# Two small router operations on VectorE move to the end of steps 5 and 7

## The reference, cut to what matters

```
x = x + window_attention(group_norm(x))     # 16 images of 256 tokens, 16 heads of 32
t = t + attention(layer_norm(t))            # the same 16 x 256 tokens, 8 heads of 16
t = t + experts(layer_norm(t))              # 8 experts, each token uses 2

# in experts, the router:
logits = x @ router_w.T + router_b
topk_val, topk_idx = top_k(logits, 2)
weights = softmax(topk_val)
onehot = one_hot(topk_idx, 8)
cw = einsum('btk,btke->bte', weights, onehot)
```

## Time and profile before

| | |
|---|---|
| median of 3 executions | 775.05 us (773.21 to 776.81) |
| the profiled execution | 776.03 us |
| its span, first to last instruction | 774.2 us |
| busy: PE, PEld, DVE, ACT, POOL | 646.9, 546.3, 515.2, 503.8, 483.6 us |
| mean granted TensorE clock | 0.953 of full speed |

### The profile page before, as it was taken

One profiled execution on the slowest core, in us unless ns is written; L12 is line 12 of the kernel. 1 busy time (PEld: TensorE's weight loads), 2 busy tenths in 40 slices (PEclk: granted clock), 3 DMA queues, 4 the chain that ended last, 5 costly groups with the idle time before them and its releaser, 6 DMA issues. The chain is left out here.

```text
span 774.2 us, 20293 instructions
## 1 busy us (share of the span) xinstructions
PE 646.9 (84%) x7070; PEld 546.3 (71%) x7070; DVE 515.2 (67%) x1513; ACT 503.8 (65%) x1427; POOL 483.6 (62%) x556
## 2 busy tenths in 40 slices
PE   3887989998989989899898999978884799999910
PEld 2766877877878778787787877767663688888800
DVE  4666768778787787887878878775342446565512
ACT  2555888778877788877888777765540256666600
POOL 5354656665868677686776767667365336666645
PEclk9799999999999999999999999999997789999965
DMA  7102113032230322303223031230732213233247
GB/s 202 29 3 35 17 21 96 11 91 35 76 98 25 91 42 82 89 34 92 42 82 87 30 97 36 85 83 36 206 122 97 65 43 93 87 88 88 73 137 215
DMA packets 54218, 59.27 MB, mean 77 GB/s; under 512 B 10370, under 2 KB 49410, under 8 KB 53602
## 3 DMA queue, kind: packets, MB, share of 16 engines
q1 hardware_dynamic: 44918, 45.65, 23.0%
q0 software_dynamic: 4544, 9.38, 3.4%
q10 hardware_dynamic: 4656, 2.95, 1.4%
HBM read 36.00 MB, written 28.64 MB: 83 GB/s over the span
## 5 line engine op out<-in xcount | busy, mean ns | idle before, releaser
L566 POOL TENSOR_TENSOR pb<-pb,rcb 128x512 f32<-128x512 f32 x128 | 155.5, 1215 | 151.7 <-DVE rcb L859 150.4
L614 POOL DMA_INDIRECT ysl<-yo,dst x78 | 75.4, 967 | 61.1 <-DVE yo L1133 44.4
L725 ACT ACTIVATE pb<-pSB,mxb 128x256 f32<-128x256 f32 x128 | 59.5, 469 | 46.4 <-DVE mxb L959 45.8
L725 ACT ACTIVATE pb<-pSA,mxb 128x256 f32<-128x256 f32 x128 | 59.6, 475 | 41.2 <-DVE mxb L959 41.2
L574 POOL TENSOR_TENSOR pa<-pa,rca 128x512 f32<-128x512 f32 x64 | 67.2, 1051 | 28.5 <-DVE rca L1024 28.5
L1252 PE MATMUL pTB<-ident,pb 128*128 128x128 f32 x512 | 79.4, 278 | 4.9 <-ACT ptb L739 4.8
L739 ACT ACTIVATE ptb<-pTB 128x512 f32<-128x512 f32 x128 | 77.1, 602 | 1.6 <-PE pTB L1252 1.6
L500 POOL DMA_INDIRECT slots<-rec,slot x64 | 65.3, 1020 | 13.8 <-issue 13.7
L745 ACT ACTIVATE pta<-pTA 128x512 f32<-128x512 f32 x64 | 38.6, 604 | 39.1 <-PE pTA L1344 38.6
L1252 PEld LDWEIGHTS pTB<-ident,pb 128*128 128x128 f32 x512 | 57.4, 141 | 9.0 <-issue 6.6
L959 DVE TENSOR_REDUCE mxb<-pSB 128x2 f32<-128x512 f32 x64 | 43.8, 685 | 20.3 <-PE pSB L1221 20.2
(11 more groups left out here) (221 smaller groups left out, 2015.3 us busy)
## 6 DMA issues: line engine op xcount, KB each, us to landing
slots<-sel_dram SPq DMA_DIRECT2D x16, 1040.0 KB
kbd<-kst SPq DMA_DIRECT2D x128, 64.0 KB, 2.4
xt<-slots SPq DMA_DIRECT2D x39, 130.0 KB, 2.2
xch<-x_ch_dram SPq DMA_DIRECT2D x4, 512.0 KB, 7.0
xt<-x_tok_dram SPq DMA_DIRECT2D x16, 128.0 KB, 2.4
xch<-t SPq DMA_DIRECT2D x16, 128.0 KB, 2.1
fw<-f_dram SPq DMA_DIRECT2D x1, 2048.0 KB
yc<-ysl SPq DMA_DIRECT2D x8, 256.0 KB, 9.4
```

What stands on the lines that cost most here:

```text
L566: pool.tensor_tensor(pb[:, b, :, :], pb[:, b, :, :], rcb[:, b, :].unsqueeze(2).to_broadcast([128, 2, TOK]), ALU.mult).then_inc(sb_nrm, 1)
L614: pool.indirect_dma_start(ysl, bass.IndirectOffsetOnAxis(ap=dst[:, t % YB, n:n + 1], axis=0), yo[:, t % YB, n, :], None).then_inc(y_dma[t ...
L725: last = a.activation(pb[:, b, qc, :], (pSB, pSA)[n % 2][:, qc * TOK:(qc + 1) * TOK], ACT.Exp, bias=mxb[:, b, qc:qc + 1], accum_out=smb[:, ...
```

## The change

On VectorE, in the function `iteration`, two blocks are moved and nothing else is touched. The comparison that makes `chose` stood at the start of step 5 and now stands at its end; the addition that makes `rden` stood at the start of step 7 and now stands at its end.

```
--- before.py
+++ after.py
@@ -875,16 +875,6 @@
                         for s in range(2):
                             last = v.max_index(ix8[:, s, :], mx8[:, s, :], lg[:, s, :])
                         last.then_inc(q_top, 1)
-                    if L is not None and n == 5:
-                        v.wait_ge(q_top, L.j * 3 + 2)
-                        if K is not None:
-                            v.wait_ge(q_mine, K.j + 1)
-                        v.tensor_tensor(chose[:, :, :, :], iota[:, :].unsqueeze(1).unsqueeze(1).to_broadcast([128, 2, 2, E]),
-                                        ix8[:, :, 0:2].rearrange("p s k -> p k s").unsqueeze(3).to_broadcast([128, 2, 2, E]),
-                                        ALU.is_equal).then_inc(q_top, 1)
-                    if L is not None and n == 7:
-                        v.wait_ge(q_exp, L.j + 1)
-                        v.tensor_scalar(rden[:, :, :], rexp[:, :, :], 1.0, None, ALU.add).then_inc(q_den, 1)
                     if K is not None and n == 0:
                         v.wait_ge(q_both, K.j + 1)
                         wait(v, q_pos, K.j)
@@ -1031,6 +1021,16 @@
                     if R is not None and n == 5:
                         v.wait_ge(r_ag, R.j + 1)
                         v.tensor_scalar(rs2[:, :], mv2[:, :, 1], EPS, None, ALU.add).then_inc(r_eps, 1)
+                    if L is not None and n == 5:
+                        v.wait_ge(q_top, L.j * 3 + 2)
+                        if K is not None:
+                            v.wait_ge(q_mine, K.j + 1)
+                        v.tensor_tensor(chose[:, :, :, :], iota[:, :].unsqueeze(1).unsqueeze(1).to_broadcast([128, 2, 2, E]),
+                                        ix8[:, :, 0:2].rearrange("p s k -> p k s").unsqueeze(3).to_broadcast([128, 2, 2, E]),
+                                        ALU.is_equal).then_inc(q_top, 1)
+                    if L is not None and n == 7:
+                        v.wait_ge(q_exp, L.j + 1)
+                        v.tensor_scalar(rden[:, :, :], rexp[:, :, :], 1.0, None, ALU.add).then_inc(q_den, 1)
```

## The result

| | before | changed |
|---|---|---|
| median | 774.48 us (22 runs) | 769.09 us (22 runs) |
| the profiled execution | 776.03 us | 765.13 us |
| its span | 774.2 us | 763.3 us |

The ratio to the kernel before is 0.9948, 95% interval 0.9931 to 0.9965: 4.0 us (2.7 to 5.3) of 774.5 are saved. One of the 22 executions of the kernel before took 1066.86 us and does not count in the ratio. 772.0 was forecast, 3.0 us less than the 775.05 of before, and "within 0.5%" as the likeliest; the measured ratio lies just beyond that edge, and its interval holds both sides of it.

The account below looks back on a forecast made before the run. VectorE's waits for GpSimd stall TensorE, but the key DMAs from `kst` to step 0 bound or nearly bound. 1.5 + 1.0 + 0.5 = 3.0 us off 776.03 gives 773.0, on the median 772.0; range 766 to 778.5.

Parts of the forecast that it names:

- within 0.5%: Whole kernel: a time not to be told from no change, between 771.2 and 778.9 us; chance 0.60.
- What bounds the kernel: VectorE's `chose` and `rden` wait for GpSimd; from `kst` to step 0 key DMAs bound or are within 0.4 us.
- Step 5, start: The cast inherits `chose`'s wait: 0.09 us gained per steady pass, 1.0 in all, and 0.5 in the first full pass.
- Step 5, end: `chose`, issued 0.01 to 0.02 us before GpSimd's next multiplication, gets through in about 0.17 us at no cost.
- Rival 3: End of step 5: `chose` waits for one multiplication (778 us, chance 0.08) or two (790 us, chance 0.05).
- Step 7: `q` starts earlier, TensorE regains 0.54 us a pass, but only the key DMAs' room of 1.5 us in sum counts.
- Step 0: `rden` pushes L893 to 0.02 us behind GpSimd's start; if caught it waits 1.04 us, hidden by the wait for TensorE.
- The sum: Whole kernel: 1.5 + 1.0 + 0.5 = 3.0 us saved, giving 772.0 us on the median.
- the forecast's own case: Whole kernel: 772.0 us, own range 770 to 774 from the late landings; chance 0.48.
- Rival 2: Step 0: key DMAs are not the bound in executions without late landings; 8.0 us saved, 767 us; chance 0.10.
- rival 1: Step 5: the cast does not exclude GpSimd, `kst` moves by some 0.8 us; 9.3 us saved, 766 us; chance 0.13.

Follow-up runs that it names:

- f3: The kernel before with four of the eight key DMAs, heads 4 to 7 getting no keys; ratio to the kernel before 0.9914.
- f4: The changed kernel with four of the eight key DMAs, heads 4 to 7 getting no keys; ratio to the kernel before 0.9786.
- g5: The changed kernel with the cast moved from step 5 into step 0 of the next pass, between the two sums; ratio to the kernel before 1.0078.
- h10: The changed kernel with the cast in step 0 of the next pass and `chose` in step 6 behind `tn`; ratio to the kernel before 0.9845.
- f2: The kernel before with only `chose` moved, `rden` at its old place; ratio to the kernel before 1.0008, 11 passes 356.4 us.
- g6: The changed kernel with one tiny VectorE reduction ahead of `chose`, so that it is issued about 0.07 us later; ratio to the kernel before 1.0025.
- f1: The kernel before with only `rden` moved, `chose` at its old place; ratio to the kernel before 0.9973, 11 passes 355.7 us.
- g7: The changed kernel with the last of the eight key DMAs issued by ScalarE instead of SyncE; ratio to the kernel before 0.985.

## Why the prediction was right, point by point

- **What bounds the kernel.** The two readings on which it stood held: small two-input or one-input SBUF operations of VectorE stand and wait for GpSimd, and the keys' DMAs bound step 0. Together they are why a change that would be worth 15 us by TensorE's stalls alone brings 4. The cast keeps most of the stall for `t` (0.65 us of 0.72 in the pass shown), and the DMAs take back most of the 0.54 for `q`. The runs f3 and f4 show the second directly.
- **Step 5, start.** The cast inherited the wait as said, 1.01 us. The Trainium skill's rule (SBUF — State Buffer, "Who interferes with whom") held for it; the waits through three operations in g5 and h10 are longer than the one instruction that it names. The gain per steady pass was put at 0.09 and was 0.12 by the profile of f2 (1.3 in 11). In the first full pass, 0.5 was put down from TensorE's idle time and 0.8 came: the term that was most mis-sized. Behind `chose` ScalarE had waited as well, 0.67 us, for the maximum `mxb` at 151.87, and TensorE another 0.15 for `t1l`; both waits went.
- **Step 5, end.** `chose` came first by 0.014 to 0.017 us in all 12 passes and cost nothing. Rival 3 is real (g6 and g5). For one wait it had put `kst` 0.42 us later and the passes 3 us above before; in g6 `kst` came 0.51 later and the passes were 2.6 us above.
- **Step 7.** `rden` took 0.15 us, TensorE's 0.54 went. Room of 1.5 us was counted for it; f1 gave 2.0. Left out of the sum was the first pass of the drain (from `kst` at 512.7 to the next at 541.8): 0.7 us shorter with `rden` moved, in f1 and in the changed kernel alike.
- **Step 0.** L893 (L883 now) was put 0.02 us behind GpSimd's start, where it might lose. It comes up to 0.01 us ahead of it in 11 of 12 passes and gets through: that it was not caught more often is luck of a hundredth of a microsecond. At 191.94, 0.03 behind the start at 191.91, it waited 1.04 us, hidden as said:

```profile
191.74 0.16 DVE L881 TENSOR_TENSOR ahead<-ahead,both 128x8 f32<-128x8 f32 x1
191.94 1.04 DVE L883 TENSOR_TENSOR ahead<-ahead,both 128x8 f32<-128x8 f32 x1
```

- **The sum.** 3.0 us were forecast; the profiles show 3.2 + 0.8 + 0.7 = 4.6 (rounded) and the timed runs 4.0 (2.7 to 5.3). The terms were each a little small. The median of 769.09 lies in the stated range of 766 to 778.5, but below the 770 to 774 given for the forecast's own case. Rival 2 (no DMA bound) was wrong, and so was rival 1. The 0.8 us a pass that rival 1 counted on came only in h10, with the cast and `chose` both at other places.

## What to carry to other kernels

A tiny VectorE operation that lasts 1 us is a wait for GpSimd, and taking it away only hands the wait to the next operation of that kind in line; look which one that is, and put the group where GpSimd idles, not where VectorE does. Before counting a removed stall, follow the longest DMA chain across the same stretch: a stall behind its start is worth only the chain's slack. An order tuned to a few hundredths of a microsecond can lose more by a speed-up elsewhere than by a slow-down, so check each small operation's distance to GpSimd's next start after every move.

## What the runs showed of the hardware

- The race between the engines is sharp. Of the operations moved here, and of `ahead`, those whose issue lay 0.02 us ahead of GpSimd's recorded start up to 0.01 us behind it all got through. `ahead`, 0.02 to 0.03 behind, waited 1.04 us, once in the changed kernel and once in each of the nine other runs that have `rden` at its new place; the 12 `chose` of g6, 0.06 behind, waited about as long. To be ahead isn't enough where GpSimd is still at work on the operation before: in g5 `chose` lay 0.06 ahead of `t1b` (318.56), but within the indirect DMA that ended at 318.53, and waited.
- How long the loser waits is open. In g6 `chose` waits for one multiplication, though GpSimd's next follows at once; in g5 it waits for three operations in a row (2.84 us), and at 564.30 in the kernel before for two. In the latter two, the wait began within 0.1 us of the end of one of GpSimd's indirect DMAs. That is not what decides: in h10 `rs` began to wait 0.5 us behind the end of one (465.23) and waited for three operations as well.
- Key DMAs of 64 KB each landed 2.4 us after issue as a rule, but in four of the 11 passes the last took 3.0 to 3.4 us in the kernel before. In g7, which issues it 0.64 us sooner, it took 3.6 to 4.0 and landed no sooner. What delays it in these passes isn't shown.
